# Two 16-head attentions: the turn of the second group of probabilities stands ahead of all four products with V

## The reference

```python
x = x + L0_xattn(ctx, layernorm(x), mask)            # 8 heads, keys from context and latents
x = x + L0_ffn(layernorm(x))                         # up to 3 steps with chosen features
x = x + L1_xattn(layernorm(x), ctx, ctx, key_mask)   # 16 heads of 8, 120 keys
x = x + L1_ffn(layernorm(x))                         # MLA (16 heads of 8, causal) and 8 experts
```

```python
scores = einsum('bhsd,bhtd->bhst', Q, K) * 8 ** -0.5  # masked
attn = softmax(scores, axis=-1)
x = einsum('bhst,bhtd->bhsd', attn, V)
out = x.transpose(...) @ w_o
```

## Time and profile before

| engine | busy us | share of the span | instructions |
|---|---|---|---|
| PE | 1232.4 | 88% | 13722 |
| PEld | 882.8 | 63% | 13722 |
| DVE | 964.3 | 69% | 2172 |
| ACT | 764.4 | 54% | 2005 |
| POOL | 568.8 | 41% | 582 |

### The profile page before, as it was taken

How to read it: one execution, slowest core, us unless ns; L and a number is a source line. 1 busy time by engine, 2 the same in 40 slices (tenths; PEclk the granted TensorE clock), 3 DMA queues, 4 the chain that set the end, 5 groups by cost and what they waited for, 6 DMA issues and landing times. The chain is left out here.

```text
span 1403.6 us, 38151 instructions
## 1 busy us (share of the span) xinstructions
PE 1232.4 (88%) x13722; PEld 882.8 (63%) x13722; DVE 964.3 (69%) x2172; ACT 764.4 (54%) x2005; POOL 568.8 (41%) x582
## 2 busy tenths in 40 slices
PE   1799999999999949811499999869999979999998
PEld 0466666666666634311388888748888867777775
DVE  5467767676767745676399999859999983443332
ACT  1587887878788722200266666536666643333332
POOL 3586656666565640000332222163333323433333
PEclk9899999999999989955599999969999998999999
DMA  8000000000000000000000000010000000000000
GB/s 211 6 2 1 0 0 0 0 0 0 0 0 0 1 1 0 0 0 1 11 12 9 9 10 9 4 61 2 0 0 0 0 3 1 11 14 7 7 7 16
DMA packets 22736, 14.65 MB, mean 10 GB/s; under 512 B 6378, under 2 KB 21610, under 8 KB 22540
## 3 DMA queue, kind: packets, MB, share of 16 engines
q1 hardware_dynamic: 22520, 13.75, 3.7%
q10 hardware_dynamic: 148, 0.01, 0.0%
HBM read 11.66 MB, written 2.10 MB: 10 GB/s over the span
## 5 line engine op out<-in xcount | busy, mean ns | idle before, releaser
L684 POOL TENSOR_TENSOR r_norm<-ssm,mhalf 128x24 f32<-128x24 f32 x32 | 134.8, 4212 | 162.1 <-DVE ssm L589 162.1
L1744 ACT ACTIVATE hid<-psum 128x512 f32<-128x512 f32 x128 | 76.3, 597 | 136.7 <-PE psum L1692 136.7
L527 ACT ACTIVATE l_probs<-psum,l_n_max 128x248 f32<-128x248 f32 x256 | 117.0, 480 | 57.5 <-DVE l_n_max L607 57.5
L1805 DVE TENSOR_TENSOR prod<-psum,combine 128x512 f32<-128x512 f32 x64 | 44.3, 692 | 144.0 <-PE psum L1702 143.7
L1836 POOL TENSOR_TENSOR acc<-acc,prod 128x512 f32<-128x512 f32 x64 | 81.1, 1268 | 147.1 <-DVE prod L1805 147.1
L1702 PEld LDWEIGHTS psum<-w,hid 128*128 128x128 f32 x1024 | 123.1, 192 | 26.8 <-issue 26.8
L1702 PE MATMUL psum<-w,hid 128*128 128x128 f32 x1024 | 123.4, 275 | 0.0
L1692 PE MATMUL psum<-moe_hT,w 128*128 128x512 f32 x256 | 122.2, 605 | 0.0
L1565 POOL TENSOR_TENSOR l_QX<-l_qT,l_own_slots 128x512 f32<-128x512 f32 x32 | 33.3, 1040 | 147.6 <-ACT l_qT L1440 147.6
L691 POOL TENSOR_TENSOR qkn<-qk,r_norm 128x1536 f32<-128x1536 f32 x32 | 88.3, 2761 | 2.5
L1565 POOL TENSOR_TENSOR mla_QX<-mla_qT,mla_own_slots 128x512 f32<-128x512 f32 x32 | 33.3, 1040 | 135.4 <-ACT mla_qT L1440 135.4
(11 more groups left out here) (309 smaller groups left out, 3387.8 us busy)
## 6 DMA issues: line engine op xcount, KB each, us to landing
X<-x_in SPq DMA_DIRECT2D x8, 256.0 KB, 5.0
out_dram<-acc SPq DMA_DIRECT2D x32, 64.0 KB, 1.5
CT<-ctx_in SPq DMA_DIRECT2D x8, 240.0 KB, 6.2
l_cT<-ctxT_in SPq DMA_DIRECT2D x32, 60.0 KB, 1.8
w<-w_in SPq DMA_DIRECT2D x1, 1024.0 KB, 5.1
wm<-wm_in SPq DMA_DIRECT2D x1, 768.0 KB, 4.2
wp<-wp_in SPq DMA_DIRECT2D x1, 768.0 KB, 6.7
wkv<-wkv_in SPq DMA_DIRECT2D x1, 512.0 KB, 5.3
```

The costliest lines, as they stand in the source:

```text
L527: e = act.activation(probs[u][:, h, :], psum[:, 2 * u + h // 2, (h % 2) * K:(h % 2 + 1) * K], ACT.Exp, bias=n_max[u][:, h:h + 1], accum_ou ...
L684: pool.tensor_tensor(r_norm[:, :], ssm[:, :], mhalf[:, 0:3 * H], ALU.pow).then_inc(s["norm_inverted"], 1)
L1744: act.activation(hid[i % RING][:, :], psum[:, 2 + i % BANKS, :], ACT.Silu).then_inc(activated[i], 1)
```

## The change

In TensorE's `body` the call `turn_group(n, par, 1)` moves up by two lines. Before, it stood between the second and the third product of entry n - 1; after, it stands between `project_qkv` and the first product. Nothing else is changed.

```diff
                     turn_group(n - 1, 1 - par, 2)
                     project_qkv(n + 1, 1 - par)
+                    turn_group(n, par, 1)
                     multiply_v(n - 1, 1 - par, 0)
                     multiply_v(n - 1, 1 - par, 1)
-                    turn_group(n, par, 1)
                     multiply_v(n - 1, 1 - par, 2)
                     multiply_v(n - 1, 1 - par, 3)
                     scores(n + 1, 1 - par)
```

## The result

The changed kernel takes 1451.61 us (median of 4 runs, 1450.3 to 1454.01), the one before 1404.23 (4 runs). The ratio is 1.0338, 95% interval 1.032 to 1.0356: slower by 47.4 us. Forecast were 1451.7 us and a range of 1439 to 1464. The profiled execution took 1450.87 us with a span of 1449.2, 45.6 more than before.

The account below looks back on a forecast made before the run. A ring from exp_a through group 1's turn and the bias to the next exp_a was taken to bound the changed kernel: L1 +22.9, MLA +24.2, together +47.1 us, giving a median of 1451.7 us; range 1439 to 1464.

Parts of the forecast that it names:

- The ring: Both attentions: exp_a to turn of group 1, to bias, to next exp_a; lengthens by 0.74 (L1), 0.82 us (MLA); 85%.
- the wait that appears: TensorE, free 1.30 us after exp_a's start, must wait for its end; turn starts 2.17 us after that start in L1.
- From turn to bias: TensorE: four products instead of two lie between group 1's turn and the next scores' bias; 2.47 us instead of 1.59.
- From bias to exp_a: From the bias matmuls to the next exp_a: unchanged, 2.79 us in L1 and 2.87 in MLA.
- Both ways: Bias to next exp_a, through VectorE's V copy and maximum, or through scores, group 0's turn and ScalarE's copy; lengths unchanged.
- Periods: Time per entry: 7.43 us against 6.69 in L1, 7.56 against 6.74 in MLA.
- VectorE's copy of group 1: Needs product 1 done; starts 1.80 us after the turn and stays hidden by 0.26 us before the copy of V.
- The rival that made it a second limit: VectorE's group 1 copy more than 0.26 us late, excess paid 62 times; 0.2 us more gives 1464 us; 6%.
- TensorE's pause: TensorE idle 0.9 to 1.0 us ahead of the turn of group 1 in nearly every entry.
- The clock: TensorE's granted clock stays at 1.00 despite the pauses; rival: half the entries at half clock, 1582 us; 3%.
- The faster rival: TensorE saves two changes between turns and products, 0.22 us an entry, if exp_a is no limit; 1391 us; 3%.
- the bounds: Wait of 0.05 or 0.19 us: +8.7; shorter time from turn to product: -6.8; reading of starts: give or take 6.

Follow-up runs that it names:

- The early signal: Changed order, but ScalarE takes heads 4 to 7 first and the turn of group 1 waits for these only; 1402.88 us, ratio 0.9984 to the kernel before.
- half the move: Against the kernel before, the turn of group 1 stands between products 0 and 1 in both stages; 1424.4 us, ratio 1.0142.
- pauses of 1.46 us: Against the kernel before, the turn of group 1 goes ahead of the next entry's three projections as well; 1499.82 us, ratio 1.0683.
- both waits gone: Changed order, with ScalarE doing heads 4 to 7 and 0, copies of q and group 2, then heads 1 to 3; 1393.29 us, ratio 0.9925 to the kernel before.
- two of the experiments: Changed order with heads 4 to 7 first and signalled early, 1402.88 us; old kernel with the turn moved between products 2 and 3, 1444.76 us.
- the old order and the split exp_a: Kernel before, with ScalarE doing heads 4 to 7 and 0, copies of q and group 2, then heads 1 to 3; 1403.02 us, ratio 0.9991.
- the early signal in the old order: Kernel before, with heads 4 to 7 first and the turn of group 1 waiting for these only; 1404.84 us, ratio 1.0003.

## Why the prediction was right

The ring held: the wait that appears, its length and what closes it behind were as worked out. That the median lies within 0.1 us of the forecast is in part luck, as single runs spread over 3.7 us and the two stages together grew by 46.7 us in the profiled execution.

- *The wait.* Forecast: the turn starts 0.05 us after exp_a's end. It does, 803.15 to 803.20. The early signal took the wait away, and with it the whole loss.
- *From turn to bias.* Forecast 2.47, measured 2.47; half the move gave 2.02 where 2.03 was worked out.
- *From bias to exp_a.* Forecast unchanged at 2.79, measured 2.78. Both ways kept their length.
- *Periods.* Forecast 7.43 and 7.56, measured 7.42 and 7.56. Stage sums: forecast 22.9 and 24.2, measured 22.70 and 24.01.
- *VectorE's copy of group 1.* Forecast to be hidden by 0.26 us, with 0.62 to the next work. It started 1.80 us after the turn as worked out, and VectorE was idle for another 0.18 us before the copy of V, which is less than 0.26 because the copy took its full 0.69. From the busy times of rows 1 and of the first table above, VectorE's idle time grew by about 0.6 us an entry in L1 and 0.7 in MLA, where about 0.7 was forecast. The rival that made it a second limit did not come.
- *TensorE's pause.* Forecast 0.9 to 1.0 us; the records show 0.80 in L1, which is outside, and 0.90 in MLA. Start to start it is 1.18 in L1 where 0.22 is usual, that is 0.96: the bracket is smaller because the modelled end of the last projection reaches into the pause.
- *The clock.* Stayed at 1.00, here and with pauses of 1.46 us.
- *The faster rival.* It was put at 1391 under the condition that exp_a ends earlier. The condition was not met in the changed kernel. But it was not the whole condition: with the turn's wait alone gone the time was 1402.9, because product 2 was still held, and only with both waits gone was it 1393.3. Of its price of 0.22 us an entry the runs gave 0.24 in L1 and 0.10 in MLA, together 9.7 us of 13.6.
- *What the prediction left out.* The second ring, by the copy of group 2 to product 2. It did no harm, as the change moves product 2 away from that copy (it starts at 804.68, the copy ends at 803.79). It decided two of the experiments. In MLA before the change it was just as long as the period: 2.86 from exp_a to product 2 (1039.94 to 1042.80), 1.01 to the bias and 2.87 back are 6.74, and that was the period. It cost next to nothing there: with the old order and the split exp_a, which opens this ring, the period is 6.72.
- *What it read wrongly.* The 0.22 us of rows 2 were taken as the turn standing behind exp_a, and the 2.31 us from exp_a to the turn as part of a ring that sets the period. The turn can start 2.17 us after exp_a does, so this ring had 0.14 us to spare; the early signal in the old order changed nothing. The forecast used the 2.17 and is not touched by it.
- *The range.* Its lower end, 1439, adds both the 6.8 and the 6 us of the bounds; its upper end of the ring, 1461, adds the 8.7 without the 6. Added alike it would be 1466.

## What to carry to other kernels

An instruction moved up in an in-order queue takes everything that it is moved past behind its own wait. So look first at when its input is ready, not at where it would fit: if the input ends just before the present place, the step is already as early as it can be, and what stands ahead of it is the cover. Then follow what is behind it: when it leads back to the input of the next round, the price is paid in full in each round, here 0.74 to 0.82 us times 62. Write down every way from that input through the queue, not the first one found: the way by the copy to product 2 decided two experiments. And if the order is right by itself, make the input earlier first; the two edits together brought 11 us, while alone the one cost 47 and the other brought 1.5, hardly clear of nothing.

## What was not expected of the hardware

- Going from matmuls of one tile shape to those of another takes about 0.1 us more, start to start: 0.33 from a product (120*32) to a turn (128*120) or to the bias (32*32) where 0.22 is usual, 0.32 from the last projection to a product, but 0.22 to 0.24 from a projection to a turn in L1. That the shape is the reason is read from these starts and not tested. It is worth some 10 us over the two stages, and this showed only when no wait stood over it.
- VectorE looked full in MLA, 29.84 of 30 us at a period of 6.74. In the fastest kernel it shows 29.83 of 30 us at a period of 6.62:

```profile
1040.94 0.43 PE L1382 MATMUL psum<-mla_bias,ident_bf 32*32 32x512 bf16 x16
...
1047.56 0.43 PE L1382 MATMUL psum<-mla_bias,ident_bf 32*32 32x512 bf16 x16
```

  The same instructions took 0.12 us less. In the trace before, some of them stand further apart without idle time in brackets (1.20 us from max_a to the next instruction instead of 1.13). A busy share near 1 did not mean that the engine set the pace at 6.74; at 6.62 it may, as the exponentials wait for it there.
- A pause of 0.8 to 1.5 us in every 7.4 to 8.2 us, kept up for 200 us, did not lower TensorE's granted clock.
